# A fused attention and MoE block: softmax shares split in row layout, turned by a DMA, and run further ahead

## The reference

```python
x = x + tanh(g_xattn) * xattn(layernorm(x), ctx)     # 32 x 128 x 512
x = x + tanh(g_ffn)   * ffn(layernorm(x))            # 8 experts, top 2, and a shared MLP
# xattn: 16 heads, keys of 64 numbers, rope on the context
q_r    = einsum('bshq,hqr->bhsr', q_big, W_qr)
k_r    = einsum('bld,hdr->bhlr', kv_rope, W_kr)
attn   = softmax(einsum('bhsr,bhlr->bhsl', q_r, k_r))
ctx_c  = einsum('bhsl,bld->bhsd', attn, kv_rope)
out    = einsum('bhsd,hkd->bshk', ctx_c, w_kc_kv).reshape(b, s, H * K) @ Wo.T
```

## Time and profile before

| | us |
|---|---|
| median of 3 runs | 2038.41 (2034.86 to 2039.94) |
| the profiled execution, its own time | 2040.83 |
| its span in the profile | 2039.0 |
| granted TensorE clock over the span | 0.99 of full speed |
| PE busy over the span | 1962.0 |

### The profile page before, as it was taken

How to read it: one execution, slowest core, us unless ns; L and a number is a source line. 1 busy time by engine, 2 the same in 40 slices (tenths; PEclk the granted TensorE clock), 3 DMA queues, 4 the chain that set the end, 5 groups by cost and what they waited for, 6 DMA issues and landing times.

```text
span 2039.0 us, 32958 instructions
## 1 busy us (share of the span) xinstructions
PE 1962.0 (96%) x12313; PEld 1122.1 (55%) x12484; DVE 954.1 (47%) x1947; ACT 673.9 (33%) x1905; POOL 569.5 (28%) x651
## 2 busy tenths in 40 slices
PE   7799999999999999879999999999999999999999
PEld 7466666666666666444445555555554444444444
DVE  5666666666666665546633222222223423233243
ACT  4555555555555566521012222222210000000000
POOL 4533333333333354300022433433303110110101
PEclk9899999999999999999999999999999999999999
DMA  9212222222222232141328999989953521221202
GB/s 291 82 50 60 65 61 60 60 60 60 66 65 60 76 117 60 37 127 39 105 59 187 229 252 213 218 217 218 210 115 123 113 75 42 83 83 26 78 16 88
DMA packets 292134, 216.49 MB, mean 106 GB/s; under 512 B 225200, under 2 KB 231088, under 8 KB 292016
## 3 DMA queue, kind: packets, MB, share of 16 engines
q1 hardware_dynamic: 280496, 177.04, 33.8%
q0 software_dynamic: 11520, 37.76, 6.6%
HBM read 113.02 MB, written 48.23 MB: 79 GB/s over the span
## 4 chain that ended last, share of the span: by engine, by line
PE 88%; DVE 5%; ACT 2%; issue 2%; POOL 1%; DMA 1%; SPq 1%; DVEq 0%; POOLq 0%; ACTq 0%
PE o L575 15%; PE score L724 11%; PE p_bank L631 8%; PE o L809 8%; PE score L798 7%; PE o L735 5%; PE p_bank L724 5%; PE m_bank L724 5%; PE c_bank L588 4%; PE p_bank L798 4%; PE m_bank L798 4%; DVE arena L1005 3%; PE c_bank L735 3%; PE t_bank L735 3%; PE score L609 2%
## 5 line engine op out<-in xcount | busy, mean ns | idle before, releaser
L575 PE MATMUL o<-arena 128*128 128x512 bf16 x1473 | 341.0, 381 | 22.0 <-DVE arena L1005 18.4
L575 PEld LDWEIGHTS o<-arena 128*128 128x128 bf16 x1536 | 146.4, 99 | 183.5 <-DVE arena L1005 28.8
L1368 POOL TENSOR_TENSOR arena<-arena 128x512 f32<-128x512 f32 x128 | 133.3, 1042 | 395.1 <-DVE arena L1021 393.4
L849 ACT ACTIVATE arena<-score,arena 128x128 f32<-128x128 f32 x512 | 180.9, 365 | 175.4 <-DVE arena L1045 175.4
L724 PE MATMUL score<-arena 128*128 128x512 bf16 x1036 | 233.7, 379 | 1.1
L631 PE MATMUL p_bank<-arena 128*128 128x256 bf16 x1536 | 182.4, 276 | 0.0
L724 PEld LDWEIGHTS score<-arena 128*128 128x128 bf16 x1056 | 103.3, 98 | 124.3
L1005 DVE TENSOR_TENSOR arena<-arena 128x512 bf16<-128x512 f32 (+2 forms) x219 | 153.2, 709 | 23.1 <-ACT arena L904 8.6
L809 PE MATMUL o<-arena 128*128 128x512 bf16 (+1 forms) x681 | 160.0, 379 | 2.1
L631 PEld LDWEIGHTS p_bank<-arena 128*128 128x128 bf16 x1536 | 147.3, 99 | 25.1 <-issue 0.7
L798 PE MATMUL score<-arena 128*128 128x352 bf16 x960 | 151.5, 315 | 2.9 <-issue 2.9
(11 more groups left out here) (162 smaller groups left out, 2929.5 us busy)
## 6 DMA issues: line engine op xcount, KB each, us to landing
xrow_d<-arena SPq DMA_DIRECT2D x80, 256.0 KB, 3.6
arena<-w_expert SPq DMA_DIRECT2D x32, 544.0 KB, 5.2
arena<-w_shared SPq DMA_DIRECT2D x22, 384.0 KB, 3.5
arena<-x SPq DMA_DIRECT2D x16, 512.0 KB, 4.5
arena<-x SPq DMA_DIRECT2D x32, 256.0 KB, 2.8
x_d<-arena SPq DMA_DIRECT2D x32, 256.0 KB, 2.2
xn_d<-arena SPq DMA_DIRECT2D x32, 256.0 KB, 2.2
arena<-x_d SPq DMA_DIRECT2D x8, 1024.0 KB, 5.7
```

What stands on the lines that cost most here:

```text
L575: mm = pe.matmul(o_bank[b % 2][:, :], lhsT=cT[:, a, h, :], rhs=M_w[:, w, head_of(hg, h), :], start=(hg == 0 and n == 0), stop=(hg == 3 and ...
L849: mm = act.activation(prob[:, u % 4, h, :], score_bank[u % 2][:, h * S:(h + 1) * S], ACT.Exp, bias=neg_max[:, u % 4, h:h + 1], accum_out=d ...
L1368: pool.tensor_tensor(prob[:, u % 4], prob[:, u % 4], rden[:, u % 4, :].unsqueeze(2).broadcast_to([P, 4, S]), ALU.mult).then_inc(normed, 1)
```

## The change

The softmax shares are no longer transposed by PE. ACT casts the normalised `prob` to a high part `share[HI]`, POOL subtracts it for the low part, and one DMA transpose per step, issued by SP, turns both parts (128 x 1024 bf16) into one of four `pT` buffers. The scores run six steps ahead of `o` and no longer four, the context two steps ahead and no longer one, in two banks by turns (`c_bank` and `t_bank`, which the transposes leave free), with two `cT` buffers. The residual `x1` has four buffers and is loaded eight steps earlier. ACT and DVE have a written order for even and odd steps. The splits of the shared MLP's weights, one in each of twelve steps before, are one in every second of 24. The scores' wait on the pieces keeps its formula though the scores are two steps earlier.

```diff
 # SP
+                u = k + 3
+                if within(u, NU):
+                    wait(sp, share_lo, u + 1, 16, it)
+                    sp.dma_start_transpose(pT[u % 4].rearrange("p l (h n) -> p (l h) n", h=4),
+                                           share[u % 2].rearrange("p l n -> p (l n)")).then_inc(pT_in[u % 4], 16)
...
 # PE
-                u = k + 1
+                u = k + 2
                 if within(u, NU):
-                    wait(pe, pt_lo, u + 1, 16, it)
-                    wait(pe, ct_lo, u, 16, it)
+                    wait(pe, pT_in[u % 4], 16 * (u // 4 + 1), 64, it)
+                    wait(pe, ct_lo, u - 1, 16, it)
...
-                u = k + 2
-                if within(u, NU):
-                    wait(pe, normed, u + 1, 16, it)
-                    wait(pe, pt_lo, u, 16, it)
-                    for h in range(4):
-                        mm = pe.transpose(t_bank[:, h * S:(h + 1) * S], prob[:, u % 4, h, :], ident_sb)
-                    mm.then_inc(pt_mm, 1)
-                u = k + 4
+                u = k + 6
                 if within(u, NU) and u % 2 == 0:
...
 # ACT
+                u = k + 4
+                if within(u, NU):
+                    wait(act, normed, u + 1, 16, it)
+                    wait(act, pT_in[(u - 2) % 4], 16 * ((u - 2) // 4 + 1), 64, it)
+                    act.copy(share[u % 2][:, HI, :], prob[:, u % 4].rearrange("p h n -> p (h n)"))\
+                        .then_inc(share_hi, 1)
+                if k % 2 == 1:
+                    exps(k + 6, it)
+                u = k + 2
+                if within(u, NU):
+                    wait(act, ct_mm, u + 1, 16, it)
+                    act.copy(cT[u % 2][:, HI].rearrange("p h n -> p (h n)"), ctx_bank[u % 2][:, :]).then_inc(ct_hi, 1)
+                if k % 2 == 0:
+                    exps(k + 6, it)
+                upper_piece(k + 12, it)
...
 # POOL
+                u = k + 4
+                if within(u, NU):
+                    wait(pool, share_hi, u + 1, 16, it)
+                    pool.tensor_tensor(share[u % 2][:, LO, :], prob[:, u % 4].rearrange("p h n -> p (h n)"),
+                                       share[u % 2][:, HI, :], ALU.subtract).then_inc(share_lo, 1)
+                u = k + 5
```

More of the change, by code:

```diff
@@ L126, in build @@
         kr_at = taken[0]
[L127 to L130, removed]
+        cT_region = [words(512) for _ in range(2)]
+        cT = [halves(r).rearrange("p (l h n) -> p l h n", l=2, h=4) for r in cT_region]
+        share = [halves(k_region[:, 4096 + i * 512:4608 + i * 512]).rearrange("p (l n) -> p l n", l=2) for i in range(2)]
+        pT = [halves(k_region[:, 5120 + i * 512:5632 + i * 512]).rearrange("p (l n) -> p l n", l=2) for i in range(4)]
         neg_max = words(16).rearrange("p (u h) -> p u h", u=4)
@@ L136, in build @@
         xn1_rows = [halves(words(D)).rearrange("p (l n) -> p l n", l=2) for _ in range(2)]
-        x1 = words(2 * D).rearrange("p (b n) -> p b n", b=2)
+        x1_region = words(2 * D)
+        x1 = [r[:, i * D:(i + 1) * D] for r in (x1_region, k_region[:, 7168:8192]) for i in range(2)]
         factor_at = taken[0]
@@ L157, in build @@
         Wq_w = [halves(r).rearrange("p (l h d) -> p l h d", l=2, h=H // 2) for r in (k_region[:, 4096:], stage[:, 0:4096])]
[L158 removed]
+        assert cT_region[0].shape == cT_region[1].shape
         kr_stage = arena[:, kr_at:kr_at + H * R]
@@ L219, in piece_bank @@
         def piece_bank(q):
-            return score_bank[1] if q % 2 == 1 and q < 8 else p_bank
+            return score_bank[1] if q % 2 == 1 and q < 6 else p_bank
+        ctx_bank = [c_bank, t_bank]
         acc_bank = [o_bank[0], o_bank[1], t_bank, c_bank]
@@ L250, in build @@
                                                   sem("normed"))
-        pt_mm, pt_hi, pt_lo = sem("pt_mm"), sem("pt_hi"), sem("pt_lo")
+        share_hi, share_lo, pT_in = sem("share_hi"), sem("share_lo"), [sem(f"pT_in{i}") for i in range(4)]
         ct_mm, ct_hi, ct_lo = sem("ct_mm"), sem("ct_hi"), sem("ct_lo")
@@ L385, in step @@
                     g = k // 8 - 1
-                    for b in (2 * g + 2, 2 * g + 3):
+                    for b in (2 * g + 4, 2 * g + 5):
                         if within(b, NB):
-                            wait(sp, x1_out[b % 2], 16 * (b // 2), 32, it)
-                            wait(sp, xn2_ready, b - 1, 4, it)
-                            sp.dma_start(x1[:, b % 2, :], x[at(b, 4, it)]).then_inc(xres_in[b % 2], 16)
+                            wait(sp, x1_out[b % 2], 16 * (b // 2 - 1), 32, it)
+                            wait(sp, xn2_ready, b - 3, 4, it)
+                            sp.dma_start(x1[b % 4], x[at(b, 4, it)]).then_inc(xres_in[b % 2], 16)
                 if m in (6, 7):
@@ L601, in step @@
                     wait(pe, exped, u, 16, it)
-                    wait(pe, pr_lo, 8 if u == 0 else 8 * g + 2 * hg + 4, 16, it)
+                    wait(pe, pr_lo, 6 if u == 0 else 8 * g + 2 * hg + 4, 16, it)
                     cols = slice((b % 2) * S, (b % 2 + 1) * S)
@@ L614, in step @@
                     g, j = q // 8, q % 8
-                    wait(pe, pr_lo, q if q >= 8 else q - 1, 16, it)
+                    wait(pe, pr_lo, q if q >= 6 else q - 1, 16, it)
                     if q in (0, 1):
@@ L882, in step, with exps @@
                                  m_bank[:, 0:E].rearrange("p (o e) -> p o e", o=1)).then_inc(lg_up, 1)
-                if it is None and within(k - FFN_FIRST, 12):
-                    split_wsh(k - FFN_FIRST)
+                if it is None and (k - FFN_FIRST) % 2 == 0 and within((k - FFN_FIRST) // 2, 12):
+                    split_wsh((k - FFN_FIRST) // 2)
+            def exps(u, it):
+                if within(u, NU):
+                    wait(act, maxed, u + 1, 16, it)
+                    for h in range(4):
+                        mm = act.activation(prob[:, u % 4, h, :], score_bank[u % 2][:, h * S:(h + 1) * S], ACT.Exp,
+                                            bias=neg_max[:, u % 4, h:h + 1], accum_out=den[:, u % 4, h:h + 1])
+                    mm.then_inc(exped, 1)
             def upper_mf(h):
```

66 lines of the change are left out of this document (25 added, 41 removed).

## The result

The changed kernel takes 2054.5 us (median of 4 runs, 2050.78 to 2055.81) against 2036.63 (4 runs, 2034.63 to 2039.94): ratio of the means 1.0083, 95% interval 1.0063 to 1.0104. It is slower by 0.8%. The forecast was 2030 us, the range 1990 to 2043, the chance of slower 0.15.

What follows compares the result with a forecast made beforehand. PE set the pace before; afterwards the serial DVE and ACT chain would give back PE's savings. Rounds +2, start -1, end -9 make -8 us from the median 2038.41: 2030 us, range 1990 to 2043.

Steps and rivals of the forecast that it cites:

- PE's floor: PE without transposes and low-part waits needs 45.05 us for eight steps; as a rival 1965 us, chance 0.07.
- The chain from X to step 4's scores: DVE's and ACT's serial work from X, the start of step 7's `x1`, until step 4's scores may start: 31.2 us.
- Its steps: The chain's parts: step 0 6.65 us, step 1 9.3, step 2 5.2, step 3 4.8, step 7 up to 5.2.
- PE's own part: From step 4's scores to the next X, PE sets the pace: 18.5 us, without two transposes.
- This term, 12 x (49.7 - 49.54) = +2: Twelve rounds of eight steps, each 49.7 us where it was 49.54, cost +2 us.
- if the added instruction held nothing: Had POOL's added subtraction held no DVE link, step 1 would take 8.1 us and the round 48.5.
- The clock: Rival: the lower clock follows PE's rests in steps 2 and 4, up to 31 us, 2061 us; chance 0.1.
- A granted clock below 1.00 in the middle: Sign that would show the forecast wrong: PE's granted clock falling below 1.00 in the middle of the run.
- The start and the end: Step 0's `o` comes earlier, -1 us; steps 116 to 127, without pieces, get shorter, -9, between -3 and -13.
- DMA, residual buffers: nothing: The DMA transpose lands in time for PE and the four residual buffers change nothing: no time taken for either.
- POOL's rope runs late into step 6, nothing, but without margin: POOL's rope of step 4 delays step 6's share by about 1 us; DVE reaches step 7's `x1` with PE.
- the holds cost less: Rival: POOL holds DVE's links less or the chain has slack, rounds 48.5 to 46.3 us, 2018 to 1990; chance 0.25.

Runs made afterwards that it cites:

- e9: Changed kernel with the 17 rsqrt-chain links behind the row maxima of steps 0 and 1, four normalisations behind step 2's: 1988.0 us, ratio 0.9745.
- e2: Changed kernel with 17 rsqrt-chain links moved: 1 to 5 behind step 0's row maximum, 6 to 17 behind step 1's: 2010.5 us, ratio 0.9861.
- e10: Changed kernel with four whole-row normalisations moved from the end of step 1 to behind step 2's row maximum, links left in place: 2042.5 us, ratio 1.0020.
- e7: Changed kernel with the weight pieces of steps 1 and 3 in the miscellaneous bank, a second piece bank: 2073.8 us, ratio 1.0171.
- e1: Changed kernel with POOL's subtraction for the low part of the shares on 8 columns instead of 512 (output wrong): 2016.3 us, ratio 0.9895.
- e6: Changed kernel with unread filler matmuls on PE, eleven ahead of step 2's piece and eight ahead of step 4's scores: 2049.4 us, ratio 1.0052.
- e11: Changed kernel with the shared FFN's weight pieces loaded and split one a step from step 98, as before the change: 2050.5 us, ratio 1.0056.
- e4: Changed kernel with each DMA turn of steps 8 to 95 issued twice, the second into a buffer nobody reads: 2054.2 us, ratio 1.0077.
- e12: Changed kernel with two residual buffers in place of four: 2049.7 us, ratio 1.0053.
- e5: Changed kernel with links moved behind row maxima, two residual-row normalisations behind step 2's maximum and two low parts behind step 3's: 2014.7 us, ratio 0.9895.
- e8: Kernel before the change with the 17 links moved behind the row maxima of steps 0 and 1: 2049.4 us, ratio 1.0063.
- e3: Changed kernel with eleven unread filler matmuls on PE ahead of the weight piece of each step 2: 2055.3 us, ratio 1.0083.

## Why the prediction was wrong, point by point

- **PE's floor, 45.05 us.** Right: e9 comes to 46.03 with 0.9 of rests in it.
- **The chain from X to step 4's scores sets the round.** Right in kind. e2, e9 and e10 shorten it and the round follows; e7 takes away the wait that looks like the cause and only moves it. From X at 449.72 to the scores at 481.52 it measured 31.80 us, where I had 31.2.
- **Its steps.** Step 7 5.17 (5.2), step 1 8.94 (9.3), step 2 5.20 (5.2), step 3 4.90 (4.8), but step 0 7.59 where I had 6.65. I followed POOL's new subtraction into step 1 only. It runs across the end of step 0 as well and holds the last link there, seen in DVE's timeline and in POOL's:

```profile
409.72 1.00 DVE L1121 TENSOR_TENSOR arena<-arena 128x4 f32<-128x4 f32 x1
```

```profile
409.55 1.16 POOL L1375 TENSOR_TENSOR arena<-arena 128x512 bf16<-128x512 f32 x1 [1.17 <-ACT arena L841]
```

- **PE's own part.** 18.76 (18.5). With the chain: a round of 50.56, not 49.7. **This term, 12 x (49.7 - 49.54) = +2, is the first that failed: it measured +11.6.** The mechanism stood, one hold of 0.83 us was left out. The term is a difference of two nearly equal rounds: an error of under 2% in the round was worth 10 us, more than the -8 of the whole forecast. The sum's own figure for "if the added instruction held nothing", 48.5, is what e1 gave (48.46); against the changed kernel that is 2.1 us a round and not the forecast's 1.2, because of the hold that was missing.
- **The clock. The second step that failed**: "PE now has two rests of about 2 us in a round" was right (2.71 and 1.89), and the drop behind them was made a rival with 0.1. It came in five rounds of twelve and cost 6.5 us there, and about 4.2 more in steps 96 to 115. A granted clock below 1.00 in the middle was one of the forecast's own signs of being wrong. The drop's price was right for PE (2.5 us; I had 2.6) and twice too high for the round, since the rest in step 4 takes up half. A drop in each of these rounds, as the rival had it, never came. With the sum's own size for the round the drop alone would not have left the range; without the drop the kernel would still have been slower (e6: 1.0052).
- **The start and the end.** -1.1 (-1), right. Steps 116 to 127 gave 7.7 (9), right in size; but 5.8 of it went again between step 96 and the end, for which I had allowed 4 either way and taken nothing. The sum stopped the rounds at step 96; 4.9 of the 5.8 lie in the two and a half rounds behind it, most of it the clock. With the spreading of the MLP's weights undone (e11) the stretch to step 116 is still 2 us longer than before (126.90), so the spreading isn't the whole of it.
- **DMA, residual buffers: nothing.** Right, by e4 and e12.
- **Small slips that change nothing.** The sum's twelve rounds of 49.54 us are ten, behind one of 47.95 and one of 49.22. The first end of the rival on the holds is 2016 by its own terms (2038.4 - 1 - 9 - 12.5), not 2018.
- **"POOL's rope runs late into step 6, nothing, but without margin."** It holds: ACT waits 2.9 us for POOL in step 6 in the view of waits, PE doesn't wait for either.
- **The rival "the holds cost less"** had 0.25 on the strength that ACT's order could move POOL by tenths. It moved the other way.

Taken together, the forecast had -8 and the span grew by 15.0, 23 more: 9.6 from the round, 6.5 from the clock in steps 0 to 95, 5.8 behind them (about 4.2 of it the clock), 1.3 from steps 116 to 127.

Open: why the drop follows one rest and not the next of the same length.

## What to carry to other kernels

When a change takes work from the bound engine, write down the in-order chain of the others before anything else, and place each small operation of it in a wait, not between two waits: the same 17 links cost 3.1 us a round less behind the row maxima (e2) than where the change had left them. Where a saving leaves the bound engine with rests of 2 to 3 us in a round, its clock can take part of it back, and it matters where the next rest is. With 1.9 us of rest behind it, a piece longer by up to 1.7 us cost nothing (e11, e12) and one longer by 2.5 cost 1.3; with none behind it, 1.65 us longer cost 1.65 (e10). Where two rounds differ by less than the error of the longest chain in the sum, forecast the sign with care.

## What the runs showed of the hardware that was not expected

- In steps 0 to 95 the lower clock came behind rests of 1.84 to 2.71 us, in some of the rounds only (3 to 9 of 12 where every round had such a rest, within a run always at the same place of the round), and behind the rests of 4.4 to 4.8 us in all eleven (e7). It came once behind one of 1.40 (e5, with a rest of 0.42 just ahead), though not behind the others of 1.0 to 1.5 there, nor behind the 1.2 to 1.5 ahead of step 2's piece in e1, nor behind the 1.3 to 1.6 ahead of `o` in e8. The rests of up to 0.47 us in e9's steady rounds never had one behind them. The same 24 matmuls then take 4.06 to 5.30 us in place of 2.79.
- Filling one rest (e3), or shortening it to 1.3 or 0.4 us (e1, e2), moved the drop to the next one, of 1.84 to 1.89 us, which it hadn't followed before.
- Doubling the turns by DMA, at 0.68 of the DMA engines' time, changed no round by more than 0.05 us.
